# A fused cross-attention and mixture-of-experts kernel: the small TensorE item of each step moved behind the transposed scores, and the router arithmetic spread over four steps

## The reference, cut to what matters

```python
x = x + xattn(layernorm(x), fside, ctx)      # softmax over 512 keys, 16 heads, projections Wq, Wk, Wv, Wp
router_probs = softmax(x @ w_router)
gate_weights = softmax((x @ w_gating) / 0.1)
g, u = x @ w_gate[e], x @ w_up[e]            # 256 -> 1024, for each of 8 experts
expert_out = (silu(g) * u) @ w_down[e]       # 1024 -> 256
cw = router_probs * gate_weights
cw = cw / (cw.sum(-1) + 1e-9)
out = x + sum_e expert_out[e] * cw[e]        # x here layer-normed for the experts and the router
```

## Time and profile before

| | before |
|---|---|
| median of 3 runs | 2790.26 us (2788.6 to 2790.9) |
| the profiled execution | 2790.06 us, of which the span is 2788.0 us |
| PE busy | 98% of the span, 16416 products |
| DVE / ACT / POOL busy | 79% / 61% / 65% |
| granted TensorE clock over the span | 0.994 of full speed |
| HBM traffic | 249 MB, 89 GB/s |

### The profile page before, as it was taken

One profiled execution on the slowest core, in us unless ns is written; L12 is line 12 of the kernel. 1 busy time (PEld: TensorE's weight loads), 2 busy tenths in 40 slices (PEclk: granted clock), 3 DMA queues, 4 the chain that ended last, 5 costly groups with the idle time before them and its releaser, 6 DMA issues.

```text
span 2788.0 us, 47546 instructions
## 1 busy us (share of the span) xinstructions
PE 2723.0 (98%) x16416; PEld 2224.3 (80%) x16416; DVE 2189.3 (79%) x3254; ACT 1695.2 (61%) x3241; POOL 1813.8 (65%) x1886
## 2 busy tenths in 40 slices
PE   7789999999999999999999999999999999999998
PEld 5578878888887878878788787887878788888887
DVE  7877788778888788777787788877878778776665
ACT  7766666665666666566665666656666665544443
POOL 6766676666666667666676666766666666655554
PEclk9999999999999999999999999999999999999999
DMA  2113232332322323323222322323323233333332
GB/s 69 36 60 99 80 92 96 91 103 77 98 91 92 102 76 95 95 92 98 80 92 91 100 90 88 96 84 110 91 77 99 76 103 92 95 106 112 106 105 83
DMA packets 251275, 252.27 MB, mean 90 GB/s; under 512 B 15904, under 2 KB 242848, under 8 KB 251040
## 3 DMA queue, kind: packets, MB, share of 16 engines
q1 hardware_dynamic: 251040, 249.25, 28.8%
HBM read 240.66 MB, written 8.52 MB: 89 GB/s over the span
## 4 chain that ended last, share of the span: by engine, by line
PE 87%; DVE 7%; ACT 3%; issue 3%; POOL 1%; DMA 0%; POOLq 0%; ACTq 0%; DVEq 0%
PE ps_s L660 23%; PE ps_t L660 23%; PE ps_o L694 23%; PE ps_s L753 4%; PE ps_t L763 3%; PE ps_m L549 3%; PE ps_a L735 2%; PE ps_a L737 2%; DVE h_lo L949 2%; DVE negmax L1139 1%; PE ps_m L597 1%; PE ps_m L557 1%; DVE hf L944 1%; ACT h_hi L782 1%; DVE hf L937 1%
## 5 line engine op out<-in xcount | busy, mean ns | idle before, releaser
L949 DVE TENSOR_TENSOR h_lo<-hf,h_hi 128x512 fp32r<-128x512 f32 x512 | 506.0, 988 | 231.6 <-ACT h_hi L782 221.4
L782 ACT ACTIVATE h_hi<-hf 128x512 fp32r<-128x512 f32 x512 | 323.9, 633 | 510.6 <-DVE hf L944 510.6
L937 DVE SCALAR_TENSOR_TENSOR hf<-hf,ps_s 128x512 f32<-128x512 f32 x512 | 349.8, 683 | 278.0 <-ACT hf L777 275.2
L777 ACT ACTIVATE hf<-ps_s 128x512 f32<-128x512 f32 x512 | 305.6, 597 | 312.4 <-PE ps_s L660 204.5
L1170 POOL TENSOR_TENSOR wg_lo<-stage_w,wg_hi 128x512 fp32r<-128x512 f32 x256 | 340.0, 1328 | 224.1 <-ACT wg_hi L789 223.9
L1235 POOL TENSOR_TENSOR Pt_lo<-Pt 128x512 f16<-128x512 f32 x256 | 312.3, 1220 | 149.0 <-ACT Pt L916 148.5
L694 PE MATMUL ps_o<-h_hi,wd_hi 128*128 128x512 f32 x1024 | 399.9, 390 | 0.9 <-DVE h_lo L949 0.9
L694 PE MATMUL ps_o<-h_lo,wd_hi 128*128 128x512 f32 x1024 | 400.1, 391 | 0.0
L694 PE MATMUL ps_o<-h_hi,wd_lo 128*128 128x512 f32 x1024 | 398.5, 389 | 0.0
L1170 POOL TENSOR_TENSOR wd_lo<-stage_w,wd_hi 128x512 fp32r<-128x512 f32 x256 | 332.5, 1299 | 82.5 <-ACT wd_hi L789 82.4
L916 ACT ACTIVATE Pt<-ps_t 128x512 f32<-128x512 f32 x512 | 304.5, 596 | 124.1 <-PE ps_t L763 120.3
(11 more groups left out here) (193 smaller groups left out, 5117.0 us busy)
## 6 DMA issues: line engine op xcount, KB each, us to landing
stage_w<-in_L_ffn_w_gate_dram SPq DMA_DIRECT2D x256, 256.0 KB, 2.7
stage_w<-in_L_ffn_w_up_dram SPq DMA_DIRECT2D x256, 256.0 KB, 2.8
stage_w<-in_L_ffn_w_down_dram SPq DMA_DIRECT2D x256, 256.0 KB, 2.7
cwb<-d_cw SPq DMA_DIRECT2D x64, 256.0 KB, 3.7
X<-in_x_dram SPq DMA_DIRECT2D x32, 256.0 KB, 3.1
C<-in_fside_BxSxS_dram SPq DMA_DIRECT2D x16, 256.0 KB, 3.0
KVM<-in_ctx_dram SPq DMA_DIRECT2D x16, 256.0 KB, 2.7
d_x<-X SPq DMA_DIRECT2D x16, 256.0 KB, 2.4
```

The source lines that it names most:

```text
L777: act.activation(hf[:], ps_g[:], ACT.Tanh, scale=0.5).then_inc(tanh_done, 1)
L782: act.activation(h_hi[f % FC][:], hf[:], ACT.Copy).then_inc(hh_done, 1)
L937: dve.scalar_tensor_tensor(out=hf[:], in0=hf[:], scalar=1.0, in1=ps_g[:], op0=ALU.add, op1=ALU.mult).then_inc(gate_done, 1)
L949: dve.tensor_tensor(h_lo[f % FC][:], hf[:], h_hi[f % FC][:].bitcast(F32), ALU.subtract).then_inc(hl_done, 1)
```

## The change

On PE the misc item of a step comes last, behind `s` and `t`, where it came ahead of them. ACT takes the exponential ahead of the copy that belongs to the misc item, and DVE takes the row maximum ahead of its share of the misc item. The router arithmetic is spread: `css` and `csum` go from step 19 to 20, `cden` and `crec` from 20 to 21, `cw` from 20 to 22. `cwT` goes from step 21 to 23 and changes places with the first `y`; the DMA that writes `cwT` goes from step 22 to 24, and the reads that follow it from offsets 3 and 5 of a group of 64 expert steps to offsets 6 and 7.

```diff
@@ ITEMS
-                 (20, "kT", 1, 1), (21, "cwT", 0, -1), (22, "qq", 6, 0), (23, "y", 0, 0), (24, "y", 1, 0), (25, "kT", 2, 1),
+                 (20, "kT", 1, 1), (21, "y", 0, 0), (22, "qq", 6, 0), (23, "cwT", 0, -1), (24, "y", 1, 0), (25, "kT", 2, 1),
@@ sync
-                    if step == 22 and turn.has(-1):
+                    if step == 24 and turn.has(-1):
                         turn.wait(eng, cwT_done, -1, 1)
@@ combine_ahead
-                if at == 3:
+                if at == 6:
                     load_combine(expert)
-                if at == 5 or at % EXPERT == 3 and EXPERT < at < GROUP - EXPERT:
+                if at == 7 or at % EXPERT == 3 and EXPERT < at < GROUP - EXPERT:
@@ tensor: do_misc goes from ahead of the score product to behind the transposed scores
-                    name, k, d, one, freed = misc(turn, step)
-                    if name:
-                        do_misc(turn, name, k, d, one, freed)
-
                     d, i = item_at(step, AHEAD)
...
                                   start=True, stop=True).then_inc(t_ps.sem, 1)
+
+                    name, k, d, one, freed = misc(turn, step)
+                    if name:
+                        do_misc(turn, name, k, d, one, freed)
@@ scalar: the exponential goes from behind the misc copies to ahead of them
+                    if turn.has(0):
+                        i = step
+                        turn.wait(act, t_ps, 0, i + 1)
...
+                        act.activation(Pt[i % RING][:], key_bank(turn.b * STEPS + i)[:], ACT.Exp).then_inc(exp_done.sem, 1)
                     name, k, d, one, _ = misc(turn, step)
@@ router_weights
+                if step == 20:
                     turn.wait(dve, lsum_done, -1, 1)
                     dve.scalar_tensor_tensor(out=css[:], in0=lsum[:, :, 0], scalar=CW_EPS, in1=lsum[:, :, 1],
...
-                if step == 20:
+                if step == 21:
                     turn.wait(dve, csum_done, -1, 2)
                     dve.tensor_tensor(cden[:], css[:], csum[:], ALU.add).then_inc(cden_done.sem, 1)
...
+                if step == 22:
                     turn.wait(dve, crec_done, -1, 1)
@@ vector: the row maximum goes from behind the misc work to ahead of it
+                    d, i = item_at(step, AHEAD)
+                    if turn.has(d):
+                        turn.wait(dve, s_ps, d, i + 1)
...
                     name, k, d, one, _ = misc(turn, step)
```

More of the change, by code:

```diff
@@ L867, in body @@
                                            scale=scale).then_inc(lexp_done.sem, 1)
+                    if turn.has(0):
+                        i = step
+                        turn.wait(act, t_ps, 0, i + 1)
+                        turn.wait(act, av_ps, 0, KC * (i // KC) - RING + KC)
+                        if turn.b == 0 and i == 0:
+                            act.wait_ge(w_low, len(parts))
+                        act.activation(Pt[i % RING][:], key_bank(turn.b * STEPS + i)[:], ACT.Exp).then_inc(exp_done.sem, 1)
                     name, k, d, one, _ = misc(turn, step)
@@ L908, in body @@
                         act.activation(cwT[:], ps[0:E, 0:N], ACT.Copy).then_inc(cwT_done.sem, 1)
[L909 to L916, removed]
             turns(body)
@@ L1076, in body @@
                                           ALU.subtract).then_inc(lo_dve.sem, 1)
+                    d, i = item_at(step, AHEAD)
+                    if turn.has(d):
+                        turn.wait(dve, s_ps, d, i + 1)
+                        if i % 4 == 0:
+                            turn.wait(dve, mq_l, d, i // 4 - 1)
+                        dve.tensor_reduce(negmax[:, (i // 4) % 2, i % 4:i % 4 + 1], score_bank((turn.b + d) * STEPS + i)[:], AX.X, ALU.max,
+                                          negate=True).then_inc(max_done.sem, 1)
                     name, k, d, one, _ = misc(turn, step)
@@ L1133, in body @@
                         normalise(turn, 2, X, mv, rstd, XN, xn_done)
[L1134 to L1140, removed]
             turns(body)
```

## The result

The changed kernel took 2824.55 us (median of 4 runs, 2821.2 to 2826.9), the kernel before in the same comparison 2789.7 us: a ratio of 1.0123 with a 95% interval of 1.0111 to 1.0136, slower by some 35 us. The direction was forecast, the size was not: +9.6 us was said, and the range ended at 2814.

A forecast was written before the change was run, and what follows sets the result against it. PE, busy for 98% of the span, was taken as the bound. To 2790.06 us came +7.1 (turns with experts), +7.5 (transitions) and -5 (before 170 us): +9.6, 2799.7 us; range 2793 to 2808, full range 2773 to 2814.

The forecast's parts named there:

- the stretch before 170 us: Attention alone, before the experts: earlier exponential and `negmax` filling a wait shorten DVE's waits; half taken as gain, -5 us.
- the chain in steps 18 to 21: Later `qq` delays ACT's stack, POOL's chain and `negmax`: +0.45 us in odd turns, +0.76 in even ones.
- step 23: `cwT`'s transposes no longer hide in a wait: +0.2 us; in even turns, with `y` gone, -0.23 us.
- The DMAs: Later `cwT` write and reads on SP's queue still land before the weighing in step 26: cost 0.
- the double transition: PE steps with attention output and no other wait pay a second short-to-long transition: 0.08 us in 94 steps, +7.5 us.
- The spreading works: Rival: in step 20 DVE's `Pt_lo` gets operands ahead of POOL's, saving 1.8 us in 12 turns: 2771 us, chance 0.15.
- `css` does not wait: Rival: in step 20 `css` takes 0.15 us and `Pt_lo` runs ahead of POOL's: 2788.3 us, no change, chance 0.2.
- DVE falls behind further: Rival: waits for POOL in step 22 make step 23 or 24 wait 0.8 us in 12 turns: 2809 us, chance 0.15.

The follow-up runs named there:

- the run that undoes it: Changed kernel with the old order on PE, ACT and DVE up to step 18 of turn 2, before the experts: 2808.8 us, 1.0068.
- moving POOL's instruction: Kernel before with the stacking of the query block's copies in step 19 instead of 18: 2766.4 us, 0.9915.
- The one kernel whose trace has it both ways: Changed kernel with PE's item ahead of `s` and `t` in the eight attention-output steps, from step 19 of turn 2: 2796.2 us, 1.0027.

## Why the prediction was right and wrong

**Wrong: the stretch before 170 us, put at -5 us.** It is +18.6 us in the profiled execution, and 16 us by the run that undoes it. The prediction took half of DVE's waits as the gain and wrote "below, nothing, or a few us lost by the later `qq`". The later `qq` was most of the matter: the query blocks' steps alone give back 11 of the 16 us, and together PE and ACT all of it. I had priced it in step 18, where ACT's stack waits for it, and had not asked who waits for the copies of the other query blocks. DVE's waits were no gain either: from 30 to 188 us it waits 12.0 us for the exponentials, where it had waited 6.4. That error of 21 to 24 us explains nearly all of the distance between 2799.7 and 2824.6.

**Right: the chain in steps 18 to 21.** ACT's wait for `qq` was to be 1.6 us and is 1.66, POOL's 5.5 and is 5.76. `css` was to take 1.25 us in its new place and takes 1.24. The wait of `s` for `negmax` was to be 1.7 us and is 1.39, behind a wait of 0.23 us for `h_lo` in step 20. The sum for these steps was +0.45 us in odd turns and +0.76 in even ones, and the three steps 19 to 21 grew by 0.41 and 0.64, 6.4 us in 12 turns. For step 23, which takes `cwT` and in even turns loses `y`, +0.2 and -0.23 were said; it is +0.21 (4.79 us for 4.58) and -0.24 (4.79 for 5.03). The DMAs, put at 0, cost nothing: in neither trace does DVE wait for `cwb`, though its slowest read took 5.4 us.
The rule of the Trainium skill that was weighed there ("SBUF — State Buffer", section "Who interferes with whom") fits this trace: a `css` on 2 elements ended 0.01 us after POOL's instruction. I used it too little: `h_lo` of step 19, at the head of the chain, has two operands in SBUF as well, and takes 1.85 us behind POOL's addition for 0.69 ahead of it.

**Right in kind, a little low: the double transition.** I took 0.08 us in 94 steps, +7.5 us. Putting `qq` back gives 0.09 us a step, and the 29 steps outside 19 to 21 grew by 0.90 us a turn, 10.8 us in 12 turns. Both terms with the experts come to 14.6 us in the prediction and 17.9 in the trace.

**The rivals.** "The spreading works" is out by the run with the spreading alone. "`css` does not wait" is out by its 1.24 us. "DVE falls behind further" gave a number nearer to the result, but its mechanism, waits in steps 23 and 24, isn't there: step 23 changed only by `cwT` and `y`, and step 24 takes 4.84 us for 4.80. No case on my list had the loss before the experts.

**A root that the prediction missed.** It followed the stall back to POOL's queue and stopped at "nothing in that chain has slack". The collision of `h_lo` with the additions was in the trace of before at 857.03 us, and was the part that could be removed.

## What to carry to other kernels

When an item is moved behind others on one engine, list every one of its occurrences and who reads the result of each, also in the stages where that engine is not the bound: here a loop over two engines grew by 0.6 us on one and 0.5 us on the other, 20 times, in a stretch that cost as much as all of the rest. Look for such a loop by the time from its first product to its last copy, since a test on one engine alone showed 1 to 2.4 us of 16. And where a stall ends a chain of instructions that wait for each other's port, look at the first of them and change what it meets there; the arithmetic at the end of the chain, however small or well spread, was worth 0 to 2 us, and moving POOL's instruction 24.

## What the runs showed of the hardware

The trace of before already had DVE instructions with two operands in SBUF that ended with POOL's running one (`cden` at 865.03 us, POOL's `wu_lo` at 865.01). That their order within some 30 ns decides a turn was not expected: `h_lo` takes 0.69 or 1.85 us, with nothing between, and the turn 168.0 or 170.1. The start in the record doesn't tell the winner: against ACT's stack, DVE starts at 6.13 or 6.14 us, and POOL's second addition at 6.13 to 6.16 us in the turns that DVE wins and at 6.12 to 6.17 us in those that it loses. The one kernel whose trace has it both ways had runs from 2790.3 to 2804.9 us; no other kernel's runs were further apart than 7 us.

Nor had I expected how far the granted clock would go with the waits. Between the kernel before and the changed one PE's idle time before the experts grew by 6.9 us, the time at the lower level by 37 us, and the busy time of the same 1188 products by 11.1.
